# Cross attention: a head's sum of exponents split by GpSimd into high and low part, multiplied with ones in two one-pass products

## The reference

```python
q = (hidden_states @ Wq).reshape(B, Sq, H, D)
k = (encoder_hidden_states @ Wk).reshape(B, Skv, H, D)
v = (encoder_hidden_states @ Wv).reshape(B, Skv, H, D)
q = rmsnorm(q, gq)
k = rmsnorm(k, gk)
scores = jnp.einsum('bqhd,bkhd->bhqk', q, k) * scale
attn = jax.nn.softmax(scores, axis=-1)
out = jnp.einsum('bhqk,bkhd->bqhd', attn, v)
return out.reshape(B, Sq, H * D) @ Wo
```

## Time and profile before

| | |
|---|---|
| median of 3 runs | 2727.55 us (2721.56 to 2730.68) |
| the profiled execution | 2722.14 us, span 2720.3 us |
| TensorE (PE) busy | 2241.9 us, 82% of the span |
| VectorE (DVE) busy | 1435.5 us, 53% |
| ScalarE (ACT) busy | 1209.5 us, 44% |
| GpSimd (POOL) busy | 908.0 us, 33% |
| mean granted clock of TensorE | 0.922 of full speed |

### The profile page before, as it was taken

How to read it: one execution, slowest core, us unless ns; L and a number is a source line. 1 busy time by engine, 2 the same in 40 slices (tenths; PEclk the granted TensorE clock), 3 DMA queues, 4 the chain that set the end, 5 groups by cost and what they waited for, 6 DMA issues and landing times. The chain is left out here.

```text
span 2720.3 us, 34145 instructions
## 1 busy us (share of the span) xinstructions
PE 2241.9 (82%) x11672; PEld 1543.5 (57%) x11672; DVE 1435.5 (53%) x2135; ACT 1209.5 (44%) x2237; POOL 908.0 (33%) x554
## 2 busy tenths in 40 slices
PE   5888888857884876965899999999999999967672
PEld 4453535336763644643677767776777677734340
DVE  4656656634544435343455675557555755543435
ACT  3635354524323534532555545555555555531322
POOL 3434242410003012020455545554555555530101
PEclk9999999978896987978899999999999999988796
DMA  2000000010001000000211121112111111120001
GB/s 103 1 1 1 1 1 1 1 59 1 1 1 45 1 1 1 1 0 30 82 46 46 46 70 46 46 46 69 46 46 46 47 46 46 47 99 1 1 1 62
DMA packets 62358, 84.01 MB, mean 31 GB/s; under 512 B 6132, under 2 KB 41332, under 8 KB 61752
## 3 DMA queue, kind: packets, MB, share of 16 engines
q1 hardware_dynamic: 62264, 82.76, 9.2%
HBM read 74.36 MB, written 4.19 MB: 29 GB/s over the span
## 5 line engine op out<-in xcount | busy, mean ns | idle before, releaser
L1897 DVE RECIPROCAL s_inv_sums<-banks 128x512 f32<-128x512 f32 x64 | 214.8, 3356 | 341.6 <-PE banks L2010 338.2
L1771 POOL TENSOR_TENSOR s_qk_rstd<-s_mean_sq,minus_half 128x8 f32<-128x8 f32 x64 | 118.5, 1852 | 502.9 <-DVE s_mean_sq L1884 502.9
L591 DVE TENSOR_REDUCE s_neg_max<-banks 128x1 f32<-128x512 f32 x256 | 169.8, 687 | 114.7 <-PE banks L657 113.3
L2003 PE MATMUL banks<-s_probsT,s_v 128*128 128x512 f32 x512 | 230.2, 592 | 0.0
L1834 ACT ACTIVATE s_probsT<-banks,s_minus_bound,s_qk_rstd 128x512 f32<-128x512 f32 x256 | 177.0, 782 | 92.6 <-PE banks L200 88.6
L541 ACT ACTIVATE s_probsT<-banks 128x512 f32<-128x512 f32 x256 | 147.0, 598 | 107.2 <-PE banks L671 105.1
L198 PE MATMUL banks<-s_w_proj_hi,xT_hi 128*128 (+1 forms) x512 | 170.8, 334 | 2.9 <-DVE s_ctxT_lo L1945 2.9
L1805 ACT ACTIVATE s_squares<-banks 128x512 f32<-128x512 f32 x64 | 38.2, 597 | 285.3 <-PE banks L200 285.2
L2003 PEld LDWEIGHTS banks<-s_probsT,s_v 128*128 128x128 f32 x512 | 97.0, 189 | 110.0 <-issue 107.4
L1764 POOL TENSOR_TENSOR s_w_proj_lo<-s_w_proj_raw,s_w_proj_hi 128x2048 f32 (+1 forms) x33 | 152.1, 4610 | 14.1 <-ACT s_w_proj_hi L1797 14.1
L657 PE MATMUL banks<-s_kT,s_qT 128*128 128x512 f32 x256 | 121.3, 478 | 40.6 <-DVE s_neg_max L591 24.3
(11 more groups left out here) (409 smaller groups left out, 5987.7 us busy)
## 6 DMA issues: line engine op xcount, KB each, us to landing
s_w_proj_raw<-l1x_wq SPq DMA_DIRECT2D x33, 512.0 KB, 4.9
s_w_out_raw<-l1x_wo SPq DMA_DIRECT2D x33, 512.0 KB, 4.0
s_w_proj_raw<-l1x_wk SPq DMA_DIRECT2D x33, 256.0 KB, 5.0
s_w_proj_raw<-l1x_wv SPq DMA_DIRECT2D x33, 256.0 KB, 5.3
x_all<-x SPq DMA_DIRECT2D x4, 1024.0 KB, 12.1
s_ctxT<-ctxT SPq DMA_DIRECT2D x8, 512.0 KB, 5.9
x_cur<-x_all SPq DMA_DIRECT2D x4, 1024.0 KB, 7.7
out<-x_all SPq DMA_DIRECT2D x4, 1024.0 KB, 4.3
```

The lines of the kernel that those rows point to most:

```text
L591: dve.tensor_reduce(nmax[:, h % 2, t, 0:1], ps.ap(s), AX.X, ALU.max, negate=True) \
L1771: pool.tensor_tensor(rs[:, j, :, :], ms[:, j, :, :], c.mhalf[:, 0:T * HP].rearrange("p (t h) -> p t h", h=HP), ALU.pow) \
L1897: dve.reciprocal(inv[:, h, :], pb.ap(("sum", h))).then_inc(pb.freed(("sum", h)), 1)
L2003: mm = pe.matmul(pb.ap(("o", h)), v[:, k, h * DX:(h + 1) * DX], probsT[:, h, k, :], start=(k == 0), stop=(k == T - 1))
```

## The change

GpSimd now writes the sum of a head's exponents rounded to the one-pass format (`psum_h`), subtracts it from the first partial sum, and adds the second partial sum to give the low part (`psum_l`), with a drain after each step. That is four operations of GpSimd for a head where there were two. TensorE multiplies a matrix of ones in the same format with each part, in one pass each, and accumulates both in the same bank. The ones are set by GpSimd at the start of the stage. Nothing is moved in any engine's order, and there are no new semaphores.

```diff
--- before.py
+++ after.py
@@ -1647,7 +1647,9 @@
         f_l = sb("qkT_lo", [P, 2, HP, S], F32R)
         probsT = sb("probsT", [P, HP, T, S])
         psum2 = sb("probs_pair_sums", [P, 2, S])
-        psum1 = sb("probs_sum", [P, HP, S])
+        psum_h = sb("probs_sum_hi", [P, HP, S], F32R)
+        psum_l = sb("probs_sum_lo", [P, HP, S], F32R)
+        ones = sb("ones_rows", [P, P], F32R)
         inv = sb("inv_sums", [P, HP, S])
         o_h = sb("outT_hi", [P, HP, S], F32R)
         o_l = sb("outT_lo", [P, HP, S], F32R)
@@ -1757,6 +1759,9 @@
 
         @block.gpsimd
         def _(pool):
+            pool.memset(ones[:, :].bitcast(F32), 1.0)
+            pool.drain()
+
             def lo(out, raw, hi, hi_ready, done, turn, piece=None):
 
                 pool.wait_ge(*hi_ready.after(turn, 1))
@@ -1779,7 +1784,11 @@
                         pool.wait_ge(*pb.released(y, ("e", h, T - 1)))
                         pool.tensor_tensor(psum2[:, :, :], probsT[:, h, 0:2, :], probsT[:, h, 2:4, :], ALU.add)
                         pool.drain()
-                        pool.tensor_tensor(psum1[:, h, :], psum2[:, 0, :], psum2[:, 1, :], ALU.add).then_inc(p_sum.sem, 1)
+                        pool.tensor_tensor(psum_h[:, h, :], psum2[:, 0, :], psum2[:, 1, :], ALU.add)
+                        pool.drain()
+                        pool.tensor_tensor(psum2[:, 0, :], psum2[:, 0, :], psum_h[:, h, :].bitcast(F32), ALU.subtract)
+                        pool.drain()
+                        pool.tensor_tensor(psum_l[:, h, :], psum2[:, 0, :], psum2[:, 1, :], ALU.add).then_inc(p_sum.sem, 1)
                         pool.drain()
                 if x is not None:
                     tx = x[1]
@@ -2007,7 +2016,8 @@
                 def sums(h):
                     pb.wait_empty(pe, y, ("sum", h))
                     pe.wait_ge(*p_sum.after(y, h + 1))
-                    pe.matmul(pb.ap(("sum", h)), c.ones[:, :], psum1[:, h, :], start=True, stop=True) \
+                    pe.matmul(pb.ap(("sum", h)), ones[:, :], psum_h[:, h, :], start=True, stop=False)
+                    pe.matmul(pb.ap(("sum", h)), ones[:, :], psum_l[:, h, :], start=False, stop=True) \
                       .then_inc(pb.filled(("sum", h)), 1)
 
                 def project_out(t):
```

## The result

The changed kernel takes 2874.69 us (median of 4 runs, 2864.06 to 2880.31) where the kernel before takes 2724.67 (median of 4): **ratio 1.0543, interval 1.0506 to 1.0581**. It is slower by 150 us. Its profiled execution took 2864.06 us with a span of 2862.3, 142.0 longer than the span before.

The account below looks back on a forecast made before the run. The prediction took TensorE to bound the cross stage, any standstill lengthening it one for one. 2722.1 + 117.6 (inner passes) + 24.5 (other passes) + 16 (clock) = 2880.3; with 5.4 to the median, about 2885 us, range 2848 to 2925.

Parts of the forecast that it names:

- Margins and chain: Inner pass: head sums ready 0.44 and 0.73 us early; 2.9 and 5.8 us of lateness makes the pass 38.2 us.
- Cost of an added operation: GpSimd, two more operations a head: 1.45 us each, between 1.27 and 1.52; writing the one-pass format at no extra cost.
- The waits: TensorE, inner pass: stands some 2.5 us before head 0's product with ones and 2.9 us before head 1's.
- Inner passes: 24 inner passes of the cross stage, each 4.9 us longer: 117.6 us.
- The other passes: First, turn-over and after-turn-over passes +2.8 us each, seven in all, and the last +4.9: together 24.5 us.
- the last pass: Last pass of the stage: no queries to cover anything, last reciprocal moves from 2395.63 to 2400.5, +4.9 us.
- The clock: TensorE's clock drops after a wait in two in five of 32 passes, less 3 us already paid: +16 us.
- the rival of a low clock in every pass: Rival: TensorE's clock falls in every pass, giving 2918 us; chance 0.15.
- The price of 1.5: TensorE after a wait: one drop to the lower clock costs 1.5 us of work.
- The lower end: Own forecast's low end, 2841 us: added operations at 1.27 take 23 off, quick restarts 6.
- only the first wait counts: Rival: head 1's added work lies under values(1), an inner pass loses 2.0 us, 2778 us in all; chance 0.05.
- GpSimd stays covered: Rival: the waits never end last and 26 us go, a gain to 2702 us; chance 0.03.

Follow-up runs that it names:

- Experiments 3: Changed kernel with three GpSimd operations a head in place of four, the second partial sum left out of the low part; ratio 1.0141.
- experiments 4: Changed kernel with five GpSimd operations a head in place of four, the last addition done twice; ratio 1.0835.
- experiment 9: Changed kernel with the low part of the output weights made behind the sums and SP's two load issues swapped; 2824 us, ratio 1.0356.
- experiments 5: Changed kernel with TensorE's product for head 0 moved behind values(1), right ahead of that for head 1; 2918 us, ratio 1.0707.
- experiment 10: Changed kernel with nine extra one-pass products ahead of each of TensorE's waits for a sum; 2861.93 us, ratio 1.0503.
- experiment 11: Changed kernel with the split moved from GpSimd to VectorE and the output weights' low part behind the sums, SP's issues unswapped; 2812 us, ratio 1.0326.

## Why the prediction was right

The forecast was 2885 us, 2848 to 2925; measured 2875. The mechanism held. That the number is as close as 10 us is in part luck: for the profiled execution the forecast adds up to 2880, 158 above before, and its span grew by 142.0. The inner and after-turn-over passes and the clock came out below their terms. The other runs are 10 to 16 us longer than the profiled one, which the forecast did not foresee, and that makes up the difference.

- **Margins and chain.** The reading that GpSimd's head sums are just on time, and that 5.8 us of lateness of the second, less the margin, go straight into the pass, held: the sums came 2.82 and 5.73 us later (15.12 - 12.30, 22.03 - 16.30), and the pass was 38.09 for 38.2. Experiments 3, 4 and 9 confirm it by lengthening and shortening the chain.
- **Cost of an added operation.** 1.45 us taken, 1.41 to 1.44 measured. Writing the one-pass format costs nothing, by the means of 64 operations in ns: 1278 and 1263 for the two that write it, 1271 for the one that doesn't.
- **The waits.** 2.5 and 2.9 forecast; 2.27 and 2.74 by the rows, or 2.28 and 1.04 where the clock fell between them. TensorE's share of the stage is 88%, forecast near 85%.
- **Inner passes.** 117.6 forecast; 24 x (38.09 - 33.34) = 114.0 measured, and 6.3 more in four longer ones, where the clock fell behind the second wait.
- **The other passes.** 19.6 forecast for the first seven of them, 16.1 measured: 2.9 for the first, 9.1 for the turn-overs, 4.1 for those after (8.4 less 3 forecast). Together with the inner ones that is 136.4. In the last pass the last reciprocal came 4.9 us later against the pass's low part of weights, as forecast (2538.88 - 2517.80 against 2395.63 - 2379.41), and VectorE's last addition 4.2. With that and the 1.9 ahead of the stage, the 142.0 in span are accounted for within 1 us.
- **The clock.** The most mis-sized term: +16 forecast. In the profiled execution it was 6.3 in the inner passes and 1.5 in one turn-over. The forecast had 13 falls, two in five of 32 passes, that are all paid. There were 26, of which 5 were paid: the first wait catches the fall in 21 of 28 passes, values(1) pays it out of the time to spare before the second wait, and behind the second wait of 1.0 us that is left the clock stays at full speed, in 20 of the 21. That was written as an argument against the rival of a low clock in every pass, but not put into the sum. The price of 1.5 was nearly right: 1.3 to 1.5 for four of the five, and 2.7 for one, where the granted clock was 0.50 from 2075 to 2080. The rival is the right picture where only one wait is left (experiments 5 and 9). Unprofiled runs are up to 16 us slower than the profiled one; how much of that is the clock stays open.
- **The lower end.** The text of the prediction takes 23 and 6 us off 2885, which gives 2856; its 2841 is reached only if the clock's 16 go too. Measured 2875 lies inside either way.
- **The other rivals.** That only the first wait counts fell with experiments 4 and 5: it is the second that counts, and the first is free. That GpSimd stays covered was never near: the margins were 0.44 and 0.73 us against 2.82 and 5.73.

## What to carry to other kernels

An engine that is idle two thirds of the time can still be on time by half a microsecond at the one place where it hands over: before giving it work, subtract the time at which its result is ready from the time at which it is wanted, in one pass of the loop, and add up everything that queues ahead on that engine. If a loop has two waits on the same producer, find the one that ends its chain: here that was the second, and taking the first away gained nothing. Before moving a step, look for the load that waits for it and for what is issued behind that load by the same engine.

## What was not expected of the hardware

- Idle times of 2.3 to 2.7 us on TensorE were followed by the lower clock level of 1.2 GHz in most passes (21 of 28 behind the first wait, 21 of 24 in experiment 9), more often than the two in five of the kernel before. With these times filled (experiment 10) the granted clock stayed at 1.00.
- A VectorE operation of 128x512 with two inputs in SBUF took 0.69 us alone and 2.7 us beside a GpSimd operation reading SBUF (experiment 11).
